# Masking the row-max scores of a causal attention by a VectorE minimum in PSUM instead of by TensorE mask products

## The chip, the cores and the metric
One core of one Trainium2 chip runs the whole program, a decoder stack of four layers at batch 2, sequence 1024, width 128. The metric is the device time of one execution in microseconds. Before the change it is 2020.6 us, the median of 3 runs (2019.37 to 2026.57).

## The reference, cut to what matters
Only the first attention is touched. It has 16 heads of 64 columns and runs, for each batch, each head:

```python
sim = jnp.einsum('bhid,bhjd->bhij', q, k)
causal_mask = jnp.triu(jnp.ones((n, n), dtype=bool), k=1)
sim = jnp.where(causal_mask, mask_value, sim)            # mask_value = -finfo.max
attn = jax.nn.softmax(sim.astype(jnp.float32), axis=-1)
out = jnp.einsum('bhij,bhjd->bhid', attn, v)
adj = jnp.clip(adj + jnp.eye(n), 0.0, 1.0)               # adj = attn
deg = jnp.sum(adj, axis=-1, keepdims=True)
for l in range(GNN_DEPTH):                               # 2
    h = feats @ gnn_w[l] + gnn_b[l]
    h = jnp.einsum('bij,bjd->bid', adj, h) / deg
    feats = jax.nn.gelu(h + feats, approximate=False)
out = out + (feats @ lin_w + lin_b)                      # then @ Wo and a layer norm
```

n is 1024, feats starts as v. The softmax needs the maximum of each row over the keys up to the row's own place.

## The kernel before, in words
The work is cut into 16 units, each a pair of heads of one batch; `for_units` lets each engine run its own list of instructions for a unit g (`body`), in a hardware loop over the middle six pairs of a batch. Engines meet only through semaphores. The rows of a unit are 8 tiles of 128.

A unit needs its scores twice. First with rows on the partitions, to find the row maxima (`row_scores`, `row_part` on TensorE, `row_max` on VectorE): for row tile `it` the products of Q with the keys 0 to (it+1)*128 go to PSUM, and VectorE reduces them. Then with keys on the partitions, as three products of split parts plus one that subtracts the row's maximum (`score`), for the exponentials `E` that ScalarE writes (line 486). Both use the same two PSUM buffers `ring0` and `ring1` of 1024 columns (two heads of 512; `pair(r)`). Row tiles 0 to 3 fit into one buffer and alternate; tiles 4 to 7 have two halves, the first in ring0, the second, with the diagonal block, in ring1. A part is announced by `rowmax_ready`; the part that uses the same buffer next waits for `max_done` of the reduce. So TensorE is at most two parts ahead of VectorE.

In the diagonal block the keys above the row's own place must not count. TensorE sees to that with one more product per head after the scores: identity times a 128x128 bf16 matrix that holds -1e38 above the diagonal (`identb`, `mask`, line 580), added in PSUM. For the second kind of scores it is done otherwise: VectorE takes a minimum in place in PSUM with `cap`, 3e38 where the entry stands and -1e38 where it is masked (`own_score`, line 887).

The row maxima of unit g+1 are made inside the body of unit g. TensorE's order there is written out by hand: tile 0 behind the values of the next unit, tiles 1 and 2 behind the first output mix, then the second layer's aggregations (`aggregate(F1, ...)`, line 643) with tiles 3 to 7 between them, `max_rows` (line 610: the maxima turned into a row), the first scores of the next unit (`score`, line 628), and the second layer's products (`product2`, line 695). VectorE's order is: sums and `scaled`/`out1` (lines 917, 937) with tile 0 between, `set_own` (16 instructions on the diagonal of E, line 931), tiles 1 to 5, `out2` (line 917), tiles 6 and 7, `own_score` of the next unit. For tiles 4 to 7 the two partial maxima are joined and widened by one VectorE instruction from SBUF to SBUF (`widen_high`, tile `mw`, line 879). GpSimd meanwhile runs a quotient, two bias additions and the additions of `out2`, each 128x512 (lines 356, 365, 400, 350, 371).

Of the kernel before, what the change touches and what calls it, by code (L numbers as in the profile page):

```python
# [5 lines left out]
ALU = mybir.AluOpType  # L6
# [3 lines left out]
BF16 = mybir.dt.bfloat16  # L10
# [3 lines left out]
P = 128  # L14
# [4 lines left out]
ST = SEQ // P  # L19
# [157 lines left out]
def l0_attention(nc, d, x, xnT, ident, norm):  # L177

    with ExitStack() as ctx:
        sb, pb, sem = scope(nc, ctx, "l0a")  # L180
# [6 lines left out]
        maskf = sb("maskf", [P, P])  # L187
        wo, go = sb("wo", [P, PAIRS, P]), sb("go", [P, P])
        const_in, w_in = sem("const_in"), sem("w_in")
        consts = ((maskf[:, :], d["cmask"]), (wo[:, :, :], d["wo"]), (go[:, :], d["gout"].partition_broadcast(P)),  # L190
# [5 lines left out]
        mask = sb("mask", [P, P], BF16)  # L196
        identb = sb("identb", [P, P], BF16)
# [42 lines left out]
        pool_step = sem("pool_step")  # L240
        cast_done, q_ready, k_ready, vw_ready = sem("cast_done"), sem("q_ready"), sem("k_ready"), sem("vw_ready")
# [9 lines left out]
        ua_kept, gl_kept, capped = sem("ua_kept"), sem("gl_kept"), sem("capped")  # L251
# [16 lines left out]
        def hi(h):  # L268

            return slice(h * DH, (h + 1) * DH)  # L270
# [7 lines left out]
        def pair(r):  # L278

            return ring[r][:, :].rearrange("p (h c) -> p h c", c=512)  # L280
# [21 lines left out]
        block = ctx.enter_context(nc.Block(no_gpsimd_drain=True))  # L302
# [31 lines left out]
        def _(pool):  # L334
# [3 lines left out]
            pool.wait_ge(pool_step, 2)  # L338
            pool.affine_select(out=cap[:, :], in_=cap[:, :], compare_op=ALU.is_ge, fill=-1.0e38, base=0,
                               pattern=[[1, P]], channel_multiplier=-1).then_inc(pool_step, 1)  # L340
            pool.wait_ge(const_in, NCONST)
# [203 lines left out]
        def _(pe):  # L545
            pe.wait_ge(const_in, NCONST)
            pe.wait_ge(cast_done, 6)
            pe.wait_ge(pool_step, 3)
# [24 lines left out]
            def row_part(u, it, r, c0, c1):  # L573

                for h in range(2):
                    mm = pe.matmul(pair(r)[:, h, 0:c1 - c0], QH[hi(h), it * P:(it + 1) * P], KH[hi(h), c0:c1],  # L576
                                   start=True, stop=c1 <= it * P)
                if c1 > it * P:
                    for h in range(2):
                        mm = pe.matmul(pair(r)[:, h, it * P - c0:c1 - c0], identb[:, :], mask[:, :], start=False, stop=True)  # L580
                mm.then_inc(rowmax_ready, 1)
# [262 lines left out]
        def _(dve):  # L844
            dve.wait_ge(const_in, NCONST)
            dve.wait_ge(pool_step, 3)
            dve.tensor_copy(mask[:, :], maskf[:, :]).then_inc(cast_done, 1)
            dve.tensor_copy(identb[:, :], ident[:, :]).then_inc(cast_done, 1)
# [12 lines left out]

            def row_max(u, *tiles):
                for it in tiles:
                    w = (it + 1) * P
                    if it < 4:
                        dve.wait_ge(rowmax_ready, u * NMAX + (it + 1))
                        dve.tensor_reduce(mx[:, :, it], pair(it % 2)[:, :, 0:w], AX_X, ALU.max).then_inc(max_done, 1)
                    else:
                        n = 4 + 2 * (it - 4)
                        dve.wait_ge(rowmax_ready, u * NMAX + (n + 1))  # L870
                        dve.tensor_reduce(mx[:, :, it], pair(0)[:, :, :], AX_X, ALU.max).then_inc(max_done, 1)  # L871
                        dve.wait_ge(rowmax_ready, u * NMAX + (n + 2))
                        dve.tensor_reduce(mxb[:, :, it - 4], pair(1)[:, :, 0:w - 512], AX_X, ALU.max).then_inc(max_done, 1)
                        widen_high(u, it)
# [21 lines left out]
            def first():  # L896
                keep_q_lo(0)
                keep_k_lo(0)
                row_max(0, *range(ST))
                own_score(0, 0)  # L900
# [2036 lines left out]
```

## Time and profile before
| | |
|---|---|
| median of 3 runs | 2020.6 us (2019.37 to 2026.57) |
| the profiled execution: its time, its span | 2026.7 us, 2025.0 us |
| TensorE (PE), VectorE (DVE), ScalarE (ACT), GpSimd (POOL) busy | 76%, 64%, 37%, 43% of the span |
| the first attention's row scores and maxima run | from 43 to 923 us |
| DMA | 28 GB/s on the mean |

Times in rows are microseconds from the start of the span; "mean ns of one" is the mean duration. An instruction's busy time can overlap that of its neighbour on the same engine, so the cost of one in a chain is read from start to start. A number in square brackets at a row's end is the time for which the engine was idle before it, with the instruction that released it.

### The profile page before, as it was taken

The numbers are of one execution on the slowest core, as the hardware profiler recorded it, in microseconds if no ns is written. First come the engines' busy times: TensorE is split into PE (matmuls) and PEld (weight loads), VectorE is DVE, ScalarE is ACT, GpSimd is POOL, SyncE is SP. The second block draws the span as 40 slices with busy tenths as digits, with TensorE's granted clock in tenths as the row PEclk, the third lists the DMA queues.
The fourth block names the chain that finished last, engine by engine and source line by source line (L and its number), as shares of the span: only waits on it lengthen the run. The fifth ranks groups of instructions, "written<-read, shape, count | busy, mean of one in ns | idle before, by whom it ended". The sixth has DMA issues, their size and how long they took to land. (4 is left out here: it accounts for less than half of the span.)

```text
span 2025.0 us, 25396 instructions
## 1 busy us (share of the span) xinstructions
PE 1533.3 (76%) x8233; PEld 898.2 (44%) x8233; DVE 1292.2 (64%) x2908; ACT 757.3 (37%) x1151; POOL 878.7 (43%) x574
## 2 busy tenths in 40 slices
PE   3999999999899999998666869552185736767547
PEld 2555455555555555555424546341164212222436
DVE  5567777777577777676675245677124669989514
ACT  1444444444344444544253213210021455445012
POOL 0455665566455566656200400000512028898133
PEclk9899999999999999998878759765587859888658
DMA  1000000000000000000000000005112012211232
GB/s 52 6 6 0 5 5 5 5 5 6 1 6 6 5 5 5 5 0 1 13 0 7 1 6 16 14 7 187 39 40 67 19 36 83 82 64 52 49 120 71
DMA packets 47259, 55.96 MB, mean 28 GB/s; under 512 B 8816, under 2 KB 34696, under 8 KB 46912
## 3 DMA queue, kind: packets, MB, share of 16 engines
q1 hardware_dynamic: 44272, 49.00, 8.0%
q0 software_dynamic: 2912, 6.02, 0.9%
q8 instruction: 39, 0.64, 0.1%
q14 instruction: 36, 0.29, 0.0%
HBM read 42.85 MB, written 12.15 MB: 27 GB/s over the span
## 5 line engine op out<-in xcount | busy, mean ns | idle before, releaser
L486 ACT ACTIVATE l0a_E<-l0a_ring 128x1024 f32<-128x1024 f32 x192 | 150.4, 810 | 185.9 <-DVE l0a_scrap L892 178.8
L384 POOL TENSOR_TENSOR l0a_acc<-l0a_acc,l0a_E 128x1536 f32<-128x1536 f32 (+2 forms) x96 | 201.0, 2093 | 9.1
L2602 PE MATMUL mx_ysum<-mx_hst,main_ident 128*128 128x512 f32 x256 | 143.9, 698 | 50.0 <-POOL mx_hst L2690 43.2
L2703 POOL TENSOR_TENSOR mx_dBu<-mx_XI,mx_BB 128x1024 f32<-128x1024 f32 x64 | 137.6, 2177 | 83.7 <-DVE mx_XI L2766 83.7
L643 PE MATMUL l0a_agg<-l0a_E,l0a_VH 128*64 128x512 f32 (+3 forms) x768 | 150.5, 498 | 0.1
L643 PE MATMUL l0a_agg<-l0a_E,l0a_F 128*64 128x512 f32 (+3 forms) x768 | 148.9, 505 | 0.8 <-ACT l0a_F L447 0.8
L2675 ACT ACTIVATE mx_dA<-mx_DT,mx_A 128x512 f32<-128x512 f32 x128 | 88.2, 690 | 98.8 <-DVE mx_hst L2783 98.8
L887 DVE TENSOR_TENSOR l0a_ring<-l0a_ring,l0a_cap 128x256 f32<-128x256 f32 x128 | 55.0, 430 | 108.6 <-PE l0a_ring L633 108.6
L925 DVE RECIPROCAL l0a_AT<-l0a_RB 128x128 f32<-128x128 f32 x128 | 111.9, 920 | 1.5
L2602 PEld LDWEIGHTS mx_ysum<-mx_hst,main_ident 128*128 128x128 f32 x256 | 53.9, 219 | 120.9 <-POOL mx_hst L2690 61.9
L384 POOL TENSOR_TENSOR l0a_acc<-l0a_E 128x1792 f32<-128x1792 f32 x16 | 64.4, 4024 | 81.0 <-ACT l0a_E L486 81.0
L628 PE MATMUL l0a_ring<-l0a_QH,l0a_KH 64*128 64x512 f32 (+3 forms) x384 | 81.4, 420 | 19.2 <-ACT l0a_E L486 17.4
L165 PE MATMUL n_turned<-main_ident,n_xn 128*128 128x128 f32 x96 | 26.0, 460 | 92.0 <-DVE n_xn L135 92.0
L576 PE MATMUL l0a_ring<-l0a_KH,l0a_QH 64*128 64x512 f32 (+3 forms) x384 | 80.3, 439 | 18.7 <-DVE l0a_mx L871 5.5
L2783 DVE TENSOR_TENSOR_SCAN mx_hst<-mx_dA,mx_hst,mx_dBu 128x512 f32<-128x512 f32 x64 | 82.1, 1283 | 7.5 <-DVE mx_hst L2783 0.5
L628 PEld LDWEIGHTS l0a_ring<-l0a_QH,l0a_KH 64*128 64x128 f32 x384 | 36.5, 187 | 109.7 <-ACT l0a_E L486 67.4
L371 POOL TENSOR_TENSOR l0a_S<-l0a_S,l0a_F1B 128x512 f32<-128x512 f32 x32 | 40.9, 1279 | 99.7 <-DVE l0a_S L917 99.7
L389 POOL TENSOR_TENSOR l0a_T<-l0a_VW,l0a_small 128x512 f32<-128x512 f32 x32 | 33.4, 1043 | 111.2 <-DVE l0a_small L913 111.2
L871 DVE TENSOR_REDUCE l0a_mx<-l0a_ring 128x2 fp32r<-128x1024 f32 x64 | 78.1, 1220 | 5.4 <-PE l0a_ring L576 5.4
L892 DVE SCALAR_TENSOR_TENSOR l0a_scrap<-l0a_ring,main_ident 128x128 f32<-128x128 f32 x256 | 74.6, 291 | 8.9
L576 PEld LDWEIGHTS l0a_ring<-l0a_KH,l0a_QH 64*128 64x128 f32 x384 | 35.2, 186 | 101.1 <-DVE l0a_mx L871 32.4
L2783 DVE TENSOR_TENSOR_SCAN mx_hst<-mx_dA,mx_dBu 128x512 f32<-128x512 f32 x64 | 77.4, 1210 | 2.5 <-POOL mx_dBu L2703 2.5
(493 smaller groups left out, 3764.4 us busy)
## 6 DMA issues: line engine op xcount, KB each, us to landing
mx_BB<-mx_brows SPq DMA_DIRECT2D x32, 512.0 KB, 3.6
me_W<-in_f_w SPq DMA_DIRECT2D x16, 256.0 KB
l0a_wp<-in_wqkv SPq DMA_DIRECT2D x16, 192.0 KB
moe_Wg<-in_f_wg SPq DMA_DIRECT2D x8, 256.0 KB
moe_Wu<-in_f_wu SPq DMA_DIRECT2D x8, 256.0 KB
moe_Wd<-in_f_wd SPq DMA_DIRECT2D x8, 256.0 KB
moe_Y<-rt_zeros SPq DMA_DIRECT2D x2, 1024.0 KB, 11.0
e_back<-moe_Y SPq DMA_DIRECT2D x8, 256.0 KB, 4.7
```

The lines of the kernel that those rows point to most:

```text
L384: pool.tensor_tensor(dst, src, E[:, :, ecol[jt]:ecol[jt] + w], ALU.add).then_inc(acc_done, 1)
L486: act.activation(E[:, :, at:at + n], pair(k % 2)[:, :, 0:n], ACT.Exp).then_inc(exp_done, 1)
L576: mm = pe.matmul(pair(r)[:, h, 0:c1 - c0], QH[hi(h), it * P:(it + 1) * P], KH[hi(h), c0:c1], start=True, stop=c1 <= it * P)
L628: pe.matmul(out[:, h, 0:n], a[hi(h), keys], b[hi(h), at], start=a is KH and b is QH, stop=False, skip_group_check=True)
L643: mm = pe.matmul(agg[c][cols, lo - 512 * c:512], feats[:, jt, cols], E[:, h, at + lo:at + hi], start=(jt == 0), stop=(jt == 4 * c + 3), sk ...
L871: dve.tensor_reduce(mx[:, :, it], pair(0)[:, :, :], AX_X, ALU.max).then_inc(max_done, 1)
L892: dve.scalar_tensor_tensor(scrap[:, :], pair(k % 2)[:, h, 0:P], 1.0, ident[:, :], ALU.mult, ALU.mult, accum_out=eii[:, jt, h:h + 1]).then_ ...
L925: dve.reciprocal(AT[:, t], RB[:, t]).then_inc(inv_done, 1)
L2602: mm = pe.matmul(ysum[h][:, c * 512:(c + 1) * 512], ident[:, :], hst[:, k % DEEP, c * 512:(c + 1) * 512], start=(n == 0), stop=(n == NS - ...
L2675: act.activation(dA[:, c * 512:(c + 1) * 512], DT[:, h, b * SEQ + c * 512:b * SEQ + (c + 1) * 512], ACT.Exp, scale=A[:, h, n:n + 1]).then_ ...
L2703: pool.tensor_tensor(dBu[:, k % DEEP, :], du_of(h, b), BB[:, q % 3, :], ALU.mult).then_inc(dBu_ready, 1)
L2783: dve.tensor_tensor_scan(hst[:, k % DEEP, half], dA[:, half], dBu[:, k % DEEP, half], hst[:, k % DEEP, 511:512] if c else 0.0, ALU.mult, A ...
```

## The change
The mask products are gone, with their operands: the input mask's load, the bf16 casts of mask and identity. In their place stands a matrix `rowcap` made by GpSimd at the start, and in `row_max` a VectorE minimum of the diagonal block with it (`cap_row`), followed by a wait on its own end, before the reduce of that tile.

```diff
-        maskf = sb("maskf", [P, P])
-        consts = ((maskf[:, :], d["cmask"]), (wo[:, :, :], d["wo"]), ...
+        consts = ((wo[:, :, :], d["wo"]), ...
-        mask = sb("mask", [P, P], BF16)
-        identb = sb("identb", [P, P], BF16)
+        rowcap = sb("rowcap", [P, P])
...
             pool.memset(cap[:, :], 3.0e38).then_inc(pool_step, 1)
-            pool.wait_ge(pool_step, 2)
+            pool.memset(rowcap[:, :], 3.0e38).then_inc(pool_step, 1)
+            pool.wait_ge(pool_step, 3)
...
+            pool.affine_select(out=rowcap[:, :], in_=rowcap[:, :], compare_op=ALU.is_ge, fill=-1.0e38, base=0,
+                               pattern=[[-1, P]], channel_multiplier=1).then_inc(pool_step, 1)
...
                     mm = pe.matmul(pair(r)[:, h, 0:c1 - c0], QH[hi(h), it * P:(it + 1) * P], KH[hi(h), c0:c1],
-                                   start=True, stop=c1 <= it * P)
-                if c1 > it * P:
-                    for h in range(2):
-                        mm = pe.matmul(pair(r)[:, h, it * P - c0:c1 - c0], identb[:, :], mask[:, :], start=False, stop=True)
+                                   start=True, stop=True)
                 mm.then_inc(rowmax_ready, 1)
...
-            dve.tensor_copy(mask[:, :], maskf[:, :]).then_inc(cast_done, 1)
-            dve.tensor_copy(identb[:, :], ident[:, :]).then_inc(cast_done, 1)
...
+            def cap_row(u, it, block):
+                dve.tensor_tensor(block, block, rowcap[:, :].unsqueeze(1).broadcast_to([P, 2, P]), ALU.min).then_inc(row_capped, 1)
+                dve.wait_ge(row_capped, u * ST + (it + 1))
...
                     if it < 4:
                         dve.wait_ge(rowmax_ready, u * NMAX + (it + 1))
+                        cap_row(u, it, pair(it % 2)[:, :, it * P:w])
...
                         dve.wait_ge(rowmax_ready, u * NMAX + (n + 2))
+                        cap_row(u, it, pair(1)[:, :, it * P - 512:w - 512])
                         dve.tensor_reduce(mxb[:, :, it - 4], pair(1)[:, :, 0:w - 512], AX_X, ALU.max).then_inc(max_done, 1)
```

VectorE's order before, in the body of a unit, from `set_own` (line 931) to the widening of tile 5; the three reduces of line 867 are tiles 1 to 3:

```order
L931 SCALAR_TENSOR_TENSOR l0a_E<-main_ident,l0a_small,l0a_E 128x128 x16
L867 TENSOR_REDUCE l0a_mx<-l0a_ring 128x2 x3
L871 TENSOR_REDUCE l0a_mx<-l0a_ring 128x2
L873 TENSOR_REDUCE l0a_mxb<-l0a_ring 128x2
L879 TENSOR_TENSOR l0a_mw<-l0a_mx,l0a_mxb 128x128
L871 TENSOR_REDUCE l0a_mx<-l0a_ring 128x2
L873 TENSOR_REDUCE l0a_mxb<-l0a_ring 128x2
L879 TENSOR_TENSOR l0a_mw<-l0a_mx,l0a_mxb 128x128
```

The same place in the changed kernel, to the widening of tile 4 (lines 933, 868, 872, 875 and 881 are the former 931, 867, 871, 873 and 879):

```order
L933 SCALAR_TENSOR_TENSOR l0a_E<-main_ident,l0a_small,l0a_E 128x128 x16
L859 TENSOR_TENSOR l0a_ring<-l0a_ring,l0a_rowcap 128x2x128
L868 TENSOR_REDUCE l0a_mx<-l0a_ring 128x2
L859 TENSOR_TENSOR l0a_ring<-l0a_ring,l0a_rowcap 128x2x128
L868 TENSOR_REDUCE l0a_mx<-l0a_ring 128x2
L859 TENSOR_TENSOR l0a_ring<-l0a_ring,l0a_rowcap 128x2x128
L868 TENSOR_REDUCE l0a_mx<-l0a_ring 128x2
L872 TENSOR_REDUCE l0a_mx<-l0a_ring 128x2
L859 TENSOR_TENSOR l0a_ring<-l0a_ring,l0a_rowcap 128x2x128
L875 TENSOR_REDUCE l0a_mxb<-l0a_ring 128x2
L881 TENSOR_TENSOR l0a_mw<-l0a_mx,l0a_mxb 128x128
```

A minimum now stands ahead of each reduce that holds a diagonal block; the order is otherwise the same. TensorE's order before, from tile 3 (ring1) over both halves of tile 4 to the second layer's product:

```order
L576 MATMUL l0a_ring1<-l0a_KH,l0a_QH 128x512 x2
L580 MATMUL l0a_ring1<-l0a_mask,l0a_identb 128x128 x2
L643 MATMUL l0a_agg1<-l0a_E,l0a_F1 64x512 x2
L596 REGISTER_ALU
L576 MATMUL l0a_ring0<-l0a_KH,l0a_QH 128x512 x2
L596 REGISTER_ALU
L576 MATMUL l0a_ring1<-l0a_KH,l0a_QH 128x128 x2
L580 MATMUL l0a_ring1<-l0a_mask,l0a_identb 128x128 x2
L643 MATMUL l0a_agg1<-l0a_E,l0a_F1 64x512 x2
L695 MATMUL l0a_prod<-l0a_gnn_lin,l0a_U2 128x128 x4
```

And in the changed kernel (lines 577, 641 and 693 are the former 576, 643 and 695):

```order
L577 MATMUL l0a_ring1<-l0a_KH,l0a_QH 128x512 x2
L641 MATMUL l0a_agg1<-l0a_E,l0a_F1 64x512 x2
L577 MATMUL l0a_ring0<-l0a_KH,l0a_QH 128x512 x2
L577 MATMUL l0a_ring1<-l0a_KH,l0a_QH 128x128 x2
L641 MATMUL l0a_agg1<-l0a_E,l0a_F1 64x512 x2
L693 MATMUL l0a_prod<-l0a_gnn_lin,l0a_U2 128x128 x4
```

Only the products of line 580 are gone; the parts stand where they stood.

## Rows read from the trace of the kernel before

**Rows 1.** Windows: stretch, length, busy (instructions) of PE, PEld, DVE, ACT, POOL; clock, DMA share, GB/s.
```profile
59.00:115.00 56.00, 51.22 (x314) 28.14 (x314) 31.13 (x81) 25.00 (x37) 27.72 (x16) 0.95 0.02 6
171.00:227.00 56.00, 54.05 (x342) 29.61 (x338) 40.70 (x93) 27.16 (x42) 33.99 (x21) 1.00 0.02 5
```

**Rows 2.** Grouped lines, 0 to 1000 us: busy us, mean ns, idle before.
```profile
L580 PE MATMUL l0a_ring<-l0a_mask,l0a_identb 128*128 128x128 bf16 x256 | 37.0, 227 | 0.0
```

**Rows 3.** One line's instructions (887, 879): count, ns min/median/max, first and last start.
```profile
L887 DVE TENSOR_TENSOR l0a_ring<-l0a_ring,l0a_cap x128: 405/433/433, 58.0 to 944.3; 128x256 f32<-128x256 f32 x128
...
L879 DVE TENSOR_TENSOR l0a_mw<-l0a_mx,l0a_mxb x64: 291/293/1397, 49.1 to 922.6; 128x128 fp32r<-128x128 f32 x64
```

**Rows 4.** Timeline of PE, 427 to 453.5 us: start, duration, line, operation.
```profile
438.06 0.29 PE L580 MATMUL l0a_ring<-l0a_mask,l0a_identb 128*128 128x128 bf16 x2
438.28 1.08 PE L643 MATMUL l0a_agg<-l0a_E,l0a_F 128*64 128x512 f32 x4
439.29 0.71 PE L576 MATMUL l0a_ring<-l0a_KH,l0a_QH 64*128 64x512 f32 x4
...
440.14 1.08 PE L643 MATMUL l0a_agg<-l0a_E,l0a_F 128*64 128x512 f32 x4
...
442.24 0.61 PE L576 MATMUL l0a_ring<-l0a_KH,l0a_QH 64*128 64x512 f32 x4
...
447.11 0.50 PE L576 MATMUL l0a_ring<-l0a_KH,l0a_QH 64*128 64x512 f32 x2 [0.33 <-DVE l0a_mx L871]
447.98 0.50 PE L576 MATMUL l0a_ring<-l0a_KH,l0a_QH 64*128 64x512 f32 x2 [0.36 <-DVE l0a_mxb L873]
...
452.73 0.50 PE L628 MATMUL l0a_ring<-l0a_QH,l0a_KH 64*128 64x512 f32 x2
```

**Rows 5.** Timeline of DVE, 427 to 453.5 us.
```profile
430.35 0.68 DVE L917 TENSOR_TENSOR l0a_S<-l0a_prod,l0a_small 128x512 f32<-128x512 f32 x1
431.34 0.69 DVE L937 TENSOR_TENSOR l0a_S<-l0a_S,l0a_T 128x512 f32<-128x512 f32 x1 [0.31 <-POOL l0a_T L392]
...
436.15 1.55 DVE L867 TENSOR_REDUCE l0a_mx<-l0a_ring 128x2 fp32r<-128x512 f32 x2
438.39 1.23 DVE L867 TENSOR_REDUCE l0a_mx<-l0a_ring 128x2 fp32r<-128x1024 f32 x1 [0.69 <-PE l0a_ring L580]
439.83 1.23 DVE L871 TENSOR_REDUCE l0a_mx<-l0a_ring 128x2 fp32r<-128x1024 f32 x1 [0.22 <-PE l0a_ring L576]
440.97 0.41 DVE L873 TENSOR_REDUCE l0a_mxb<-l0a_ring 128x2 fp32r<-128x256 f32 x1
441.42 1.40 DVE L879 TENSOR_TENSOR l0a_mw<-l0a_mx,l0a_mxb 128x128 fp32r<-128x128 f32 x1
442.78 1.23 DVE L871 TENSOR_REDUCE l0a_mx<-l0a_ring 128x2 fp32r<-128x1024 f32 x1
...
444.64 0.68 DVE L879 TENSOR_TENSOR l0a_mw<-l0a_mx,l0a_mxb 128x128 fp32r<-128x128 f32 x1
...
445.85 1.21 DVE L871 TENSOR_REDUCE l0a_mx<-l0a_ring 128x2 fp32r<-128x1024 f32 x1
...
451.31 0.43 DVE L887 TENSOR_TENSOR l0a_ring<-l0a_ring,l0a_cap 128x256 f32<-128x256 f32 x1 [0.47 <-PE l0a_ring L633]
451.78 0.29 DVE L892 SCALAR_TENSOR_TENSOR l0a_scrap<-l0a_ring,main_ident 128x128 f32<-128x128 f32 x1
```

**Rows 6.** Timeline of POOL, 445 to 447 us.
```profile
445.14 1.32 POOL L350 TENSOR_TENSOR l0a_VB<-l0a_VH,l0a_gnnb 128x512 f32<-128x512 f32 x1
446.42 1.26 POOL L371 TENSOR_TENSOR l0a_S<-l0a_S,l0a_F1B 128x512 f32<-128x512 f32 x1
```

**Rows 7.** Timeline of DVE, 43 to 59 us, the first preparation.
```profile
44.92 2.73 DVE L867 TENSOR_REDUCE l0a_mx<-l0a_ring 128x2 fp32r<-128x512 f32 x3 [0.87 <-PE l0a_ring L580]
...
57.97 0.43 DVE L887 TENSOR_TENSOR l0a_ring<-l0a_ring,l0a_cap 128x256 f32<-128x256 f32 x1 [1.16 <-PE l0a_ring L633]
```

More of the change, by code:

```diff
@@ L186, in l0_attention @@
         linb = sb("linb", [P, 1])
-        maskf = sb("maskf", [P, P])
         wo, go = sb("wo", [P, PAIRS, P]), sb("go", [P, P])
         const_in, w_in = sem("const_in"), sem("w_in")
-        consts = ((maskf[:, :], d["cmask"]), (wo[:, :, :], d["wo"]), (go[:, :], d["gout"].partition_broadcast(P)),
+        consts = ((wo[:, :, :], d["wo"]), (go[:, :], d["gout"].partition_broadcast(P)),
                   (gnnb[0][:, :], d["gnn_row"][0:1, :].partition_broadcast(P)),
@@ L250, in l0_attention @@
         agg1_ready, ut_kept, at_done, inv_done = sem("agg1_ready"), sem("ut_kept"), sem("at_done"), sem("inv_done")
-        ua_kept, gl_kept, capped = sem("ua_kept"), sem("gl_kept"), sem("capped")
+        ua_kept, gl_kept, capped, row_capped = sem("ua_kept"), sem("gl_kept"), sem("capped"), sem("row_capped")
         p1_ready, s1a_done, s1_done = sem("p1_ready"), sem("s1a_done"), sem("s1_done")
@@ L546, in _ @@
             pe.wait_ge(const_in, NCONST)
-            pe.wait_ge(cast_done, 6)
-            pe.wait_ge(pool_step, 3)
+            pe.wait_ge(cast_done, 4)
+            pe.wait_ge(pool_step, 5)
             def composite(u):
@@ L845, in _ @@
             dve.wait_ge(const_in, NCONST)
-            dve.wait_ge(pool_step, 3)
-            dve.tensor_copy(mask[:, :], maskf[:, :]).then_inc(cast_done, 1)
-            dve.tensor_copy(identb[:, :], ident[:, :]).then_inc(cast_done, 1)
+            dve.wait_ge(pool_step, 5)
             dve.tensor_copy(identr[:, :], ident[:, :]).then_inc(cast_done, 1)
```

## The prediction
> **What bounds the kernel now.** I read the windows first, then the grouped lines, then three timelines of one unit (TensorE, VectorE, GpSimd) side by side. The change touches only the first attention. One head pair (a "unit") takes 56.0 us there, and from 115 to 507 us every unit repeats the same pattern. In such a window TensorE is busy 54.05 of 56 us at full clock and VectorE 40.70 [rows 1]. Averages say: TensorE is the bound, VectorE has 15 us to spare. But the averages don't decide, since the changed instructions lie in one stretch of the unit, from 430 to 453 us in the unit shown. There TensorE makes the row scores of tile 5, VectorE reduces them, TensorE may overwrite the same PSUM buffer with tile 7 (or the next half), and so on: a ring of two buffers. The reader is to see in [rows 4] that TensorE, which has almost no idle time, already waits twice in this stretch for VectorE's maxima (0.33 and 0.36 us before the halves of tile 7), and in [rows 5] that VectorE works nearly without a gap: from 436.15 to 451 us its only waits of note are 0.69 and 0.22 us. Here VectorE is the bound or within 1 us of it, and it is this stretch that gets new VectorE work.
>
> **What goes.** 256 mask products (two for each of 128 tiles), 37.0 us of TensorE busy [rows 2]. Busy counts overlap: from the mask's start at 438.06 to the next product at 438.28 is 0.22 us [rows 4], so a tile gives back 0.21 to 0.22 us, 1.7 us a unit, if TensorE is what it waits for. Also gone: one load of 64 KB and two casts ahead of the first unit, beside which the start now has one memset and one affine_select on GpSimd; a few tenths each way, taken as 0 (bounds -0.5 and +0.5).
>
> **What comes.** One VectorE minimum per tile, in place in PSUM on 128x256, 128 in all, each with a wait on its own end before the reduce behind it. An instruction of the same shape and operands stands in the trace: the minimum with `cap` takes 405/433/433 ns (min/median/max of 128) and the next instruction starts 0.47 us after it (451.31 to 451.78); others do so after 0.45, so I take 0.46. Reduces without such a wait start the next one 0.09 us before they end (439.83 + 1.23 against 440.97) [rows 3, 5]. So a unit gets 8 x 0.46 = 3.7 us of VectorE work and its TensorE loses 1.7 us.
>
> The Trainium skill (VectorE: DVE Perf Modes, The DRAIN you can't avoid) says that a semaphore behind each VectorE instruction costs nothing extra over the flush that comes anyway. The two gaps above disagree by 0.12 us an instruction. By that page of the Trainium skill a cap would cost 0.34 us and, with two caps on the path behind the lock wait below, a unit some 0.24 us less and the whole 3.6 us less; I go by the row.
>
> **The chain through one unit**, all times on the clock of the unit shown [rows 4 to 6]:
> 1. Tile 0: its cap delays the product with the sums at 430.35 by 0.46, to an end at 431.49; the addition behind it stood at 431.34 waiting 0.31 us for GpSimd, so it starts near 431.42: only 0.08 us late. The row maxima of tiles 1 and 2 start at 436.15 + 0.08 = 436.23.
> 2. Tiles 1 and 2 take 0.60 and 0.87 us (1.55 for both with the overlap), with caps 0.46 more each: 438.62. Before, tile 3 could start only at 438.39, when its mask product was done; the idle 0.69 us is eaten. Tile 3: 438.62 + 0.46 + 1.23 = 440.31, before 438.39 + 1.23 = 439.62.
> 3. TensorE's second half of tile 4 needs the buffer of tile 3. It ran at about 439.7 without waiting and now starts at 440.36; behind it are the aggregation, the second layer's product and tile 5. Without the mask, and with 0.26 us for the short half (an estimate from the 0.71 us that both halves take), the aggregation starts at 440.62 instead of 440.14, and tile 5 at 442.72 instead of 442.24.
> 4. VectorE takes up tile 5 0.54 us after TensorE starts it (439.29 to 439.83, and 442.24 to 442.78), so at 443.26. Reduce 1.14, cap 0.46, reduce 0.72: the widening instruction (`mw`, line 879) comes up at 445.58 instead of 444.64.
> 5. This one has a wait that the order doesn't show. It takes 291/293/1397 ns [rows 3]: in the unit shown 1.40 us for tile 4 and 0.68 for tile 5, and both times it ends 0.18 us after a GpSimd instruction has ended (445.14 + 0.18 = 445.32 = 444.64 + 0.68). With the shift of 0.08 the GpSimd boundary lies at 445.22; the instruction now comes 0.36 us too late for it and waits for the next, 446.42 + 0.08 = 446.50, so it ends at 446.68: 1.36 us later than before. (For tile 4 the same wait works the other way: it absorbs the delay, since it was waiting anyway.)
> 6. Tile 6 starts at 445.85 + 1.35 = 447.20; first half 1.13, cap 0.46, second half 0.94: done at 449.73. TensorE's second half of tile 7 starts at 449.78, not 447.98: 1.80 late, less the mask gone behind it, 1.6 us. Everything that follows (the scores at 452.73, the exponentials, the next unit) hangs on TensorE's order and carries this on; nothing later in the unit has slack to give it back, with 1.95 us of idle in 56.
>
> What is queued behind the new waits: on VectorE the maxima themselves, on TensorE everything, since the row scores stand between aggregations in one order. GpSimd and ScalarE start later by the same amount and wait as before.
>
> **Sum.** 15 units prepare the next one's maxima: 15 x 1.6 = 24.0 us. The first preparation has nothing beside it: 3.7 us of caps, of which 0.87 us is covered by VectorE's idle time before tile 1 and 1.16 by that before its first score [rows 7]: 1.7 us. The two first units of the batches have no quotient on GpSimd, so less of step 5, but more idle on TensorE; taken at the same price. Together +25.7 us. The profiled execution took 2026.7 us, 6.1 above the median 2020.6; 2052.4 by its own time, 2046 by the median's. Bounds of a cap: from 0.34 (duration less overlap) to 0.55, near the row's 0.46, since shape and memories are the same. Those of the chain: no less than what the maxima of tile 3 force (0.4 us a unit), no more than 7 caps in line less 1.7 of masks and less the 0.9 us of idle eaten, plus one lock wait of 1.3: 1.9 us.
>
> **Rivals.**
> - *The lock wait is missed.* Step 5 rests on 0.36 us. If the widening of tile 5 catches the earlier boundary, it ends at 445.40, tile 6 starts only 0.15 us late, and what remains is two caps in tiles 6 and 7 less their masks: 0.4 us a unit, 15 x 0.4 + 1.7 = 8 us, 2029. For it: the margin is less than one cap. Against it: three independent shifts (0.08, 0.48, 0.46) add up to it. The Trainium skill (SBUF — State Buffer, Who interferes with whom) gives the mechanism: a VectorE instruction with two SBUF inputs and a GpSimd instruction that reads SBUF block each other for a whole instruction, whoever came first. By that rule the caps, with one SBUF input, are free of it; the row of 433 ns at most agrees. Chance 18%.
> - *VectorE's spare time covers it, faster.* If each tile's cap fits into the time in which TensorE does its aggregation, the masks' 128 x 0.21 = 27 us come back: 1994. For it: 54.05 busy of 56, and 15 us spare. Against it: TensorE waits for the maxima of tile 7 already. It decides at tile 3: the cap would have to end the reduce by 439.7, 0.6 us earlier than I work out. 6%.
> - *The clock falls.* The granted clock is 1.00 (2.4 GHz) in the window with 54.05 us busy; the window 59 to 115 with 51.22 busy shows 0.95, but its idle gaps lie beside work that ran at full clock [rows 1]. Gaps of 1 us each in the stretch might bring 1.2 GHz in each unit; 3 us of matrix work at that level would take up to 3 us longer, 15 x 3 = 45 more, 2091. The Trainium skill (TensorE: Matmul & The Clock Gate, A second HAM failure mode) reports a kernel in which such short idles between groups did that. 4%.
> - The minimum is as costly as said but the mask is left in place somewhere: excluded, no such product is left in this attention.
>
> **How the numbers follow.** My forecast 62%, range of its own 2040 to 2054; missed lock wait 18%, faster 6%, clock 4%, and 10% for units that settle between (2033 to 2040) or a second lock wait (up to 2062). 0.5% is 10 us, about what a measurement tells from no change. Faster 0.06; within 0.5% (up to 2031) the missed lock wait, nearly all of it: 0.17; slower 0.77. The range from 2028 to 2060 leaves out the faster case and the clock.
>
> **What would show it.** In the changed trace: units of 57.6 us; the cap at 0.43 us; TensorE waiting for the row maxima (lines of the row scores) some 3 us a unit instead of 0.7, first at the second half of tile 4; the widening at up to 1.3 us for tile 5; TensorE busy 1.7 us less a unit; clock 1.00. Wrong if units stay at 56 us or less, or if the widening of tile 5 is short.

## The result, and the profile after

The changed kernel takes 2058.03 us (median of 4, 2056.62 to 2062.06), the kernel before on the same chip 2021.13. The ratio is 1.0181, with a 95% interval from 1.0157 to 1.0205: slower by 37 us, where the sum said 26. The time lies inside the stated range of 2028 to 2060, close to its upper end, and above the 2040 to 2054 that the forecast gave as its own. The execution profiled after took 2058.1 us, with a span of 2056.4.

The first look is at the windows, the form in which [rows 1] stand: stretch, length, busy (instructions) of PE, PEld, DVE, ACT, POOL, granted clock, DMA share, GB/s. Each window here is one unit of the changed kernel, from one copy of the row sums (line 910) to the next.

```profile
380.79:438.51 57.72, 52.66 (x323) 28.75 (x323) 43.47 (x102) 27.31 (x44) 33.93 (x21) 1.00 0.02 5
321.58:380.79 59.21, 54.13 (x323) 29.25 (x323) 43.58 (x102) 27.27 (x44) 33.97 (x21) 0.97 0.02 4
694.93:755.10 60.17, 55.33 (x323) 29.83 (x323) 43.58 (x102) 27.22 (x44) 33.98 (x21) 0.94 0.02 5
```

There are three kinds of unit. The first is what the forecast worked out: 57.72 us, where the kernel before has 56.00, at full clock, with VectorE busy 2.8 us more and TensorE 1.4 us less. The second is 1.5 us longer and its clock is 0.97, the third 2.5 us longer at 0.94. I call a stretch at a granted clock of 0.50 (1.2 GHz) a dip. From the first to the last copy there are 15 units. Eleven are regular; the first of each batch, the one with the change of batch and the last one have a pattern of their own. Of the 11, five are of the first kind, four of the second, two of the third. In the kernel before all 11 are alike, between 55.96 and 56.03 us at full clock.

The timeline of PE over one undisturbed unit answers to [rows 4]; the two units lie 13.67 us apart (tile 0 of the row scores starts at 428.73 before and at 442.40 here).

```profile
445.21 1.12 PE L729 MATMUL l0a_prod<-l0a_FT,l0a_gnn_lin 128*128 128x512 f32 x2 [0.96 <-DVE l0a_S L919]
...
454.14 0.33 PE L577 MATMUL l0a_ring<-l0a_KH,l0a_QH 64*128 64x128 f32 x2 [1.00 <-DVE l0a_mx L868]
454.39 1.08 PE L641 MATMUL l0a_agg<-l0a_E,l0a_F 128*64 128x512 f32 x4
...
456.49 0.62 PE L577 MATMUL l0a_ring<-l0a_KH,l0a_QH 64*128 64x512 f32 x4
...
458.32 0.50 PE L577 MATMUL l0a_ring<-l0a_KH,l0a_QH 64*128 64x512 f32 x2 [0.20 <-DVE l0a_mx L872]
459.39 0.45 PE L577 MATMUL l0a_ring<-l0a_KH,l0a_QH 64*128 64x384 f32 x2 [0.57 <-DVE l0a_mxb L875]
...
462.18 0.50 PE L577 MATMUL l0a_ring<-l0a_KH,l0a_QH 64*128 64x512 f32 x2 [0.75 <-DVE l0a_mx L872]
463.51 0.49 PE L577 MATMUL l0a_ring<-l0a_KH,l0a_QH 64*128 64x512 f32 x2 [0.83 <-DVE l0a_mxb L875]
...
468.10 0.51 PE L626 MATMUL l0a_ring<-l0a_QH,l0a_KH 64*128 64x512 f32 x2
```

TensorE now waits 1.00 us ahead of the second half of tile 4 and 0.20 and 0.57 ahead of the halves of tile 6, where it did not wait before, and 0.75 and 0.83 ahead of the halves of tile 7, where it was 0.33 and 0.36. That makes 3.35 us of waiting for row maxima a unit instead of 0.69. The wait of 0.96 us in the first row is for sums that stand behind the minimum of tile 0 on VectorE; before, it was 0.42. The last row stood at 452.73 before; 468.10 - 13.67 is 454.43, 1.70 us later.

The timeline of DVE in the same unit answers to [rows 5]:

```profile
450.01 0.42 DVE L859 TENSOR_TENSOR l0a_ring<-l0a_ring,l0a_rowcap 128x256 f32<-128x256 f32 x1
450.46 0.69 DVE L868 TENSOR_REDUCE l0a_mx<-l0a_ring 128x2 fp32r<-128x512 f32 x1
...
456.04 0.61 DVE L881 TENSOR_TENSOR l0a_mw<-l0a_mx,l0a_mxb 128x128 fp32r<-128x128 f32 x1
457.04 1.23 DVE L872 TENSOR_REDUCE l0a_mx<-l0a_ring 128x2 fp32r<-128x1024 f32 x1 [0.38 <-PE l0a_ring L577]
...
459.37 1.03 DVE L881 TENSOR_TENSOR l0a_mw<-l0a_mx,l0a_mxb 128x128 fp32r<-128x128 f32 x1
460.32 0.68 DVE L919 TENSOR_TENSOR l0a_S<-l0a_prod,l0a_small 128x512 f32<-128x512 f32 x1
460.92 1.21 DVE L872 TENSOR_REDUCE l0a_mx<-l0a_ring 128x2 fp32r<-128x1024 f32 x1
```

and the same of POOL to [rows 6]:

```profile
457.75 2.50 POOL L351 TENSOR_TENSOR l0a_VB<-l0a_VH,l0a_gnnb 128x512 f32<-128x512 f32 x2
461.07 1.26 POOL L372 TENSOR_TENSOR l0a_S<-l0a_S,l0a_F1B 128x512 f32<-128x512 f32 x1 [0.83 <-DVE l0a_S L919]
```

The minimum takes 0.42 us and the reduce behind it starts 0.45 us after it. The widening of tile 4 (line 881) takes 0.61 us, where it was 1.40: it comes later and ends within 0.2 us of the same place. That of tile 5 comes up at 459.37 and ends at 460.40, 0.15 us after the two GpSimd instructions of which the first started at 457.75. The second of them had started at 458.98, 0.39 us before the widening came up. For the two instructions' forms over the whole run, the source view gives what answers to [rows 3]:

```profile
L859 DVE TENSOR_TENSOR l0a_ring<-l0a_ring,l0a_rowcap x128: 415/422/433, 42.6 to 960.1; 128x256 f32<-128x256 f32 x128
...
L881 DVE TENSOR_TENSOR l0a_mw<-l0a_mx,l0a_mxb x64: 291/293/1044, 50.0 to 961.8; 128x128 fp32r<-128x128 f32 x64
```

[rows 2] have no counterpart, the mask products are gone. The first preparation, on DVE, answers to [rows 7]:

```profile
43.91 0.43 DVE L859 TENSOR_TENSOR l0a_ring<-l0a_ring,l0a_rowcap 128x256 f32<-128x256 f32 x1 [0.41 <-PE l0a_ring L577]
...
59.19 0.43 DVE L889 TENSOR_TENSOR l0a_ring<-l0a_ring,l0a_cap 128x256 f32<-128x256 f32 x1 [0.56 <-PE l0a_ring L631]
```

The idle time ahead of tile 1 has shrunk from 0.87 to 0.41 us and that ahead of the first score from 1.16 to 0.56; the first score is capped at 59.19 instead of 57.97, 1.2 us later. But the row scores also started earlier in this execution, at 42.24 instead of 43.04. From there to the capped score it is 16.95 us instead of 14.93.

Where a unit is longer, windows inside it show where. In the unit that starts at 321.58:

```profile
343.00:346.70 3.70, 2.11 (x12) 0.85 (x12) 3.63 (x6) 0.60 (x1) 1.58 (x2) 1.00 0.00 0
346.70:350.10 3.40, 3.40 (x16) 1.45 (x16) 3.15 (x5) 0.00 (x0) 0.00 (x0) 0.50 0.00 0
350.10:353.60 3.50, 3.50 (x28) 2.81 (x30) 1.76 (x7) 2.18 (x3) 0.00 (x0) 1.00 0.00 0
```

The first window holds TensorE's waits for tile 7: it is busy 2.11 of 3.70 us. Right behind it TensorE works without a gap, but at 0.50, 1.2 GHz; then the clock is back.

**The account.** From the first to the last copy of the row sums the kernel before takes 864.2 us (90.18 to 954.37), the changed one 902.4 (91.65 to 994.06): +38.2. The six regular units with a dip are together 11.0 us longer than six of 57.71 would be. The other 27.2 us are 1.81 for each of the 15 units, where a regular one without a dip has 1.71. Not all of them belong to the instructions: the last unit of the 15 is 2.8 us longer than before, and it holds 9.1 us at half clock where the kernel before holds 5.4. A second profile of the changed kernel (the last run below) gives by the same working +38.3, of which 13.5 are dips of seven units and 24.8 the rest. Ahead of the first copy 1.5 us are added, so the first profile has +39.7. The spans differ by less, 31.4, since the untouched rest of the program took 1070.6 us in one profiled execution and 1062.3 in the other. It is the same code: in the eleven runs below it takes between 1059.4 and 1069.7 us. So the units are the measure here, and the medians of several runs; a pair of single spans is not.

### The profile page after: what moved, and what is told of

Read it like the earlier page. It is cut to its first block and busy times, and to the rows that moved or that the text cites. A ratio compares the mean times of both kernels' runs of the same rounds, so it can differ in the third digit from the quotient of the medians.

```text
span 2056.4 us, 25096 instructions
## 1 busy us (share of the span) xinstructions
PE 1518.6 (74%) x7977; PEld 886.7 (43%) x7977; DVE 1337.8 (65%) x3034; ACT 758.9 (37%) x1151; POOL 878.5 (43%) x576
## 5 line engine op out<-in xcount | busy, mean ns | idle before, releaser
L641 PE MATMUL l0a_agg<-l0a_E,l0a_F 128*64 128x512 f32 (+3 forms) x768 | 157.9, 532 | 0.8 <-ACT l0a_F L448 0.8
L577 PE MATMUL l0a_ring<-l0a_KH,l0a_QH 64*128 64x512 f32 (+3 forms) x384 | 81.0, 445 | 60.6 <-DVE l0a_mxb L875 21.3
```

Source lines behind the costliest of these rows:

```text
L641: mm = pe.matmul(agg[c][cols, lo - 512 * c:512], feats[:, jt, cols], E[:, h, at + lo:at + hi], start=(jt == 0), stop=(jt == 4 * c + 3), sk ...
```

## The experiments

Each kernel ran with its own profile and several timed executions beside the kernel before. "Unit" is the length of a regular unit without a dip; dips are counted in the 11 regular units of the one profiled execution. The ratio is to the kernel before on the same chip, whose median was 2021.8 us beside the runs from "neither" to "minima on tiles 4 to 7", 2025.1 beside those from "GpSimd shifted" to "neither, tensor_scalar", and 2020.1 beside the last two and "changed, again". Across these groups the ratios compare, not the medians.

| run | unit us | units with a dip | median us | ratio to before (95%) |
|---|---|---|---|---|
| before | 56.00 | 0 | 2021 | |
| changed | 57.71 | 6 | 2058.0 | 1.0181 (1.0157 to 1.0205) |
| changed, again | 57.7 | 7 | 2059.1 | 1.0191 (1.0158 to 1.0224) |
| neither | 54.93 | 0 | 2007.5 | 0.9921 (0.9902 to 0.9940) |
| both | 57.87 | 0 | 2051.8 | 1.0135 (1.0113 to 1.0157) |
| minima on tiles 0 to 3 | 57.40 | 0 | 2044.2 | 1.0119 (1.0093 to 1.0144) |
| minima on tiles 4 to 7 | 56.31 | 0 | 2033.0 | 1.0044 (1.0029 to 1.0058) |
| GpSimd shifted | 56.97 | 3 | 2053.3 | 1.0135 (1.0104 to 1.0165) |
| filler products | 57.72 | 2 | 2054.2 | 1.0150 (1.0126 to 1.0174) |
| widening by tensor_scalar | 58.01 | 0 | 2050.5 | 1.0144 (1.0116 to 1.0173) |
| neither, tensor_scalar | - | 11 | 2058.0 | 1.0163 (1.0139 to 1.0187) |
| neither, ScalarE widens | 54.32 | 0 | 1996.9 | 0.9887 (0.9863 to 0.9912) |
| minima, ScalarE widens | 57.33 | 0 | 2038.4 | 1.0089 (1.0060 to 1.0117) |

**Neither.** The two calls of the minimum are taken out of the changed kernel, so the row maxima are taken over the keys above the diagonal too. This holds for the two other kernels with "neither" as well (with tensor_scalar, and with ScalarE widening); the scores of the second kind keep their mask.

```diff
-                        cap_row(u, it, pair(it % 2)[:, :, it * P:w])
...
-                        cap_row(u, it, pair(1)[:, :, it * P - 512:w - 512])
```

> The changed kernel without its minima: neither mask products nor minima, so the row maxima include the keys above the diagonal of the last block (any bound at or above the true maximum serves the softmax). Theory A (the added time is VectorE's chain from tile 1 to tile 7, and TensorE's part of the change is a real gain of 1.7 us a unit): units of 54.6 us instead of 56.0, total 1999 us, and no dips of the granted clock in the repeated units. Rival B (VectorE's chain of maxima bounded the unit already, so products taken from TensorE bring nothing): units of 55.8 us, total 2017.

The units are 54.93 us, 1.07 shorter than before; the products were a real cost, but only two thirds of the 1.7 us came back. Of the rest, part is VectorE's: here TensorE waits for maxima four times in the stretch, 1.07 us in all, where it was 0.69 before. Rival B is refuted, and my value was 0.3 too low. The total, 2007.5, was expected at 1999.

**Both.** Mask products and minima in every tile. The diff is against the kernel before.

```diff
                 if c1 > it * P:
                     for h in range(2):
                         mm = pe.matmul(pair(r)[:, h, it * P - c0:c1 - c0], identb[:, :], mask[:, :], start=False, stop=True)
...
+                        cap_row(u, it, pair(it % 2)[:, :, it * P:w])
...
+                        cap_row(u, it, pair(1)[:, :, it * P - 512:w - 512])
```

> Mask products and minima both: TensorE as busy as before, VectorE as in the changed kernel. Theory A with the clock (TensorE's idle gaps in the changed kernel bring the dips to 1.2 GHz that cost 1.5 us each in 7 of its units): units of 57.9 us, 0.2 longer than the changed kernel's undisturbed 57.7, but no or few dips, total 2051, below the changed kernel's 2058. Rival C (the dips come by chance or from elsewhere): as many dips, total 2061.

A window of one unit:

```profile
380.60:438.47 57.87, 54.15 (x339) 29.59 (x339) 43.22 (x102) 27.26 (x44) 33.98 (x21) 1.00 0.02 5
```

TensorE does all the work that it did before, VectorE all that it does in the changed kernel, and the unit is only 0.16 us longer than the changed one: removing the products gains next to nothing once the minima are there, since TensorE then waits. With the masks the wait ahead of the first half of tile 7 is 0.34 us, where the changed kernel has 0.75; that ahead of the second half is 0.83 in both. And although a unit without a dip is longer, the kernel is faster than the changed one (1.0135 against 1.0181, intervals that just touch at 1.0157), and no regular unit has a dip: from the first to the last copy it takes 892.1 us, the changed one 902.4. That is the clock's part of the loss, shown from the other side.

**Half the tiles each.** The lists of tiles with a minimum and of tiles with a mask product are split. The diff, against the kernel before, is that of the kernel with minima on tiles 0 to 3; in the other one the two lists are exchanged. What feeds the mask products (the load and the two casts) is back in both.

```diff
-                if c1 > it * P:
+                if c1 > it * P and it in (4, 5, 6, 7):
...
+            CAPS = (0, 1, 2, 3)
...
+                if it in CAPS:
```

> Minima for row tiles 0 to 3, mask products for 4 to 7. Theory A: the four minima make the maxima of tile 3 0.7 us late, tile 5's widening arrives at 445.33 on the clock of the unit shown, misses the GpSimd boundary at 445.22 by 0.1 and ends near 446.68: unit 57.3 us (+1.3), total 2042. If it just catches the boundary: 56.4. Rival D (each minimum costs its share, half of the 1.7): 56.85 us, total 2035.

> Mask products for row tiles 0 to 3, minima for 4 to 7. Theory A: tile 4's delay is absorbed by the wait for GpSimd that its widening has anyway; tile 5's widening arrives at 445.10, just before the boundary at 445.14, and ends at 445.32 as before; what is left are the minima of tiles 6 and 7 less a mask: unit 56.25 us, total 2026. If it misses the boundary: 57.6, as the changed kernel. Rival D: 56.85 us, total 2035.

57.40 and 56.31 us against 57.3 and 56.25 expected. The totals are 2044.2 and 2033.0 against 2042 and 2026: the second is 7 us above. The unit doesn't account for that; in its profile the first unit and the one with the change of batch have dips (6.8 and 3.4 us) that the kernel before doesn't have there. Four minima cost 1.40, the other four 0.31 us, with the same instructions in the same number, and the two together are the 1.71 of the changed kernel; rival D (0.85 each) is refuted. What differs is the widening of tile 5. With the minima on tiles 0 to 3 the DVE timeline has

```profile
454.11 0.68 DVE L886 TENSOR_REDUCE l0a_mxb<-l0a_ring 128x2 fp32r<-128x512 f32 x1
454.82 1.29 DVE L892 TENSOR_TENSOR l0a_mw<-l0a_mx,l0a_mxb 128x128 fp32r<-128x128 f32 x1
```

and with those on tiles 4 to 7

```profile
450.59 0.69 DVE L886 TENSOR_REDUCE l0a_mxb<-l0a_ring 128x2 fp32r<-128x512 f32 x1
451.31 0.29 DVE L892 TENSOR_TENSOR l0a_mw<-l0a_mx,l0a_mxb 128x128 fp32r<-128x128 f32 x1
```

the same instruction, once 1.29 us and once 0.29, which is 1.00 of the 1.09 us between the two.

**GpSimd shifted.** One more GpSimd addition of 0.59 us, whose result nobody reads.

```diff
+        SHIFT = 1
...
                 if prev is not None:
+                    for _ in range(SHIFT):
+                        pool.tensor_tensor(filler[:, :], VB[:, 0, :].unsqueeze(1).broadcast_to([P, 2, P])[:, :, 0:96], VH[:, 0, :].unsqueeze(1).broadcast_to([P, 2, P])[:, :, 0:96], ALU.add).then_inc(filled, 1)
                     quotient(g, prev)
```

> The changed kernel with one more GpSimd addition (128x192, into a tile that nothing reads, about 0.6 us) ahead of the quotient, in units that have one, so that the following GpSimd instructions end 0.6 us later. Theory A (tile 5's widening waits 0.7 us because it misses a GpSimd boundary by 0.37 us): the widening of tile 5 now comes just before the boundary and takes 0.3 to 0.5 us instead of 1.03; units of 57.1 us instead of 57.7 although work was added, total 2047 with fewer dips of the clock. Rival (the widening is slow for a reason of its own): 57.7 or longer, 2058 to 2067.

Eight of the 11 regular units got shorter by 0.74 us through added work. DVE and POOL around the widening of tile 5 in one of them, and PE behind it:

```profile
457.35 0.29 DVE L886 TENSOR_TENSOR l0a_mw<-l0a_mx,l0a_mxb 128x128 fp32r<-128x128 f32 x1
```

```profile
456.13 2.64 POOL L354 TENSOR_TENSOR l0a_VB<-l0a_VH,l0a_gnnb 128x512 f32<-128x512 f32 x2
```

```profile
459.42 0.50 PE L582 MATMUL l0a_ring<-l0a_KH,l0a_QH 64*128 64x512 f32 x2
460.76 0.50 PE L582 MATMUL l0a_ring<-l0a_KH,l0a_QH 64*128 64x512 f32 x2 [0.83 <-DVE l0a_mxb L880]
```

The widening now falls between the two instructions of this pair and takes 0.29 instead of 1.03 us. The other three units (at 376.98, 637.42 and 697.97) are 59.5, 60.6 and 59.5 us long, and in each of them the same widening takes 1.41 or 1.42 us:

```profile
397.85 1.41 DVE L886 TENSOR_TENSOR l0a_mw<-l0a_mx,l0a_mxb 128x128 fp32r<-128x128 f32 x1
```

```profile
401.04 0.50 PE L582 MATMUL l0a_ring<-l0a_KH,l0a_QH 64*128 64x512 f32 x2 [1.14 <-DVE l0a_mx L877]
402.37 0.79 PE L582 MATMUL l0a_ring<-l0a_KH,l0a_QH 64*128 64x512 f32 x2 [0.83 <-DVE l0a_mxb L880]
```

It comes up 20.86 us after the start of its unit in all 11. The second GpSimd instruction of the pair starts at 20.855 to 20.864 in the three units and at 20.866 to 20.884 in the eight: a few hundredths of a microsecond decide over 1.1. That settles step 5: the wait is for the GpSimd instruction under way. The clock follows. The three units with the long widening, in which TensorE waits ahead of both halves of tile 7, are the three with a dip; the eight others have neither. The total is 6 us above what was expected, on a chip where the kernel before is some 4 us slower too; the three units are 8.6 us longer than three of 56.97, and the change of batch has a long widening and a dip as well.

**Filler products.** Products of the identity with itself, into a bank that is free, where TensorE waits: five ahead of the second half of tile 4 and three ahead of that of tile 6, though not in the first preparation.

```diff
+        FILL = {4: 5, 6: 3}
...
                         for r in range(2):
+                            if r == 1 and not (isinstance(u, int) and u == 0) and it in FILL:
+                                for _ in range(FILL[it]):
+                                    pe.matmul(turn[:, 0:P], identr[:, :], identr[:, :], start=True, stop=True)
```

> The changed kernel with products nobody reads (identity by identity, 128x128, into the bank `turn` while it is free) where TensorE waits for maxima: 5 ahead of the second half of tile 4, where it idles 1.0 us, 3 ahead of that of tile 6, where it idles 0.57. Clock theory (the dips to 1.2 GHz come from TensorE's idle gaps in this stretch): no dips, units stay at 57.7, total 2050. Rival (the dips have nothing to do with these gaps): dips as before, 2058 or above.

Units of 57.72, as expected, and two dips instead of six or seven, at a ratio of 1.0150 instead of 1.0181 and 1.0191. The gaps that were filled (1.00 and 0.57 us, now 0.28 and none) are not those right ahead of the dips, at tile 7, for which I had no free bank; these are still 0.77 and 0.83. No dips were expected, fewer are not none, and the intervals overlap: this run leans the clock theory's way and doesn't settle it.

**The widening by tensor_scalar.** Two instructions with one tensor from SBUF and a scalar pointer each. The tile `mxb` becomes plain fp32 with it.

```diff
-                dve.tensor_tensor(mw[:, it, :, :], spread(mx[:, :, it], shape), spread(mxb[:, :, it - 4], shape),
-                                  ALU.max).then_inc(mw_high, 1)
+                for h in range(2):
+                    ins = dve.tensor_scalar(mw[:, it, h, :], spread(mx[:, h, it], [P, DH]), mxb[:, h, it - 4:it - 3], None, ALU.max)
+                ins.then_inc(mw_high, 1)
```

> The changed kernel with the widening of tiles 4 to 7 written as two VectorE tensor_scalar instructions (one per head, one tensor from SBUF, the other maximum as a scalar pointer) in the place of one with two tensors from SBUF. Theory A with the lock rule: neither waits for GpSimd any more, each takes 0.17 to 0.25 us; tile 5's widening is done 0.65 us earlier, those of 6 and 7 take 0.15 us more: units of 57.2 us, total 2050. Rival (the wait is for something else than the second input): the new instructions take up to 1.3 us too, units of 57.8 us or more.

This failed: 58.01 us. The source view shows why:

```profile
L882 DVE TENSOR_SCALAR l0a_mw<-l0a_mx,l0a_mxb x128: 245/254/1321, 49.6 to 954.8; 128x64 fp32r<-128x64 f32 x128
```

These instructions can take 1.32 us as well. It is now the second one of tile 4 that does so in every regular unit, while those of tile 5 take 0.25. The rival named it rightly: one tensor input alone doesn't free an instruction. It fits what the Trainium skill says (SBUF — State Buffer, Who interferes with whom), that tensor_scalar can run in a mode that takes both ports and then contends with GpSimd; I had used only half of that rule, and no run here shows the mode itself. The total of 2050.5 agrees with the expected 2050 by luck: the units are 0.8 us longer than expected, and none has a dip. With units 0.3 us longer than in the changed kernel and TensorE no busier (52.8 us), it isn't slower than that kernel (1.0144 against 1.0181, overlapping intervals). TensorE waits 0.83 us ahead of the second half of tile 7 here but only 0.14 ahead of the first.

**Neither, tensor_scalar.** The same edit in the kernel with neither.

> Neither mask products nor minima, and the widening as two one-input instructions. Theory A: the waits for GpSimd of 0.7, 0.15 and 0.8 us (tiles 4, 5 and 6 in the kernel with neither) go; TensorE's remaining waits in the stretch shrink from 1.8 to about 1.2 us: units of 54.4 us instead of 54.93, total 2000. Rival: unchanged, 54.9 and 2007.

The worst miss of the study: 2058.0 us where 2000 was expected and 2007.5 was there without the edit. On PE:

```profile
400.00 1.04 PE L577 MATMUL l0a_ring<-l0a_KH,l0a_QH 64*128 64x512 f32 x4 [1.04 <-DVE l0a_mx L871]
...
404.28 1.66 PE L577 MATMUL l0a_ring<-l0a_KH,l0a_QH 64*128 64x512 f32 x4 [1.64 <-DVE l0a_mx L871]
```

TensorE waits 1.04 and then, in most units, 1.64 us for maxima behind widenings of up to 1.32 us, and every one of the 11 regular units has a dip of the clock (0.50 for 3.4 to 10.2 us of it); they take 58.0 to 61.3 us. The other form of four widenings a unit took the ratio from 0.9921 to 1.0163, some 49 us. A regular unit is on the mean 3.8 us longer than with neither: TensorE is busy 2.1 us more, with the same products at the lower clock, and idle 1.7 us more.

**ScalarE widens.** VectorE joins the two partial maxima by a reduce of 2x2 elements, ScalarE spreads the result.

```diff
...
-                dve.tensor_tensor(mw[:, it, :, :], spread(mx[:, :, it], shape), spread(mxb[:, :, it - 4], shape),
-                                  ALU.max).then_inc(mw_high, 1)
+                dve.tensor_reduce(mxh[:, :, it - 4], mxp[:, :, it - 4, :], AX_X, ALU.max).then_inc(joined, 1)
...
+                    act.wait_ge(joined, u * 4 + (it - 3))
+                    act.activation(mw[:, it, :, :], spread(mxh[:, :, it - 4], [P, 2, DH]), ACT.Copy).then_inc(mw_high, 1)
```

> Neither mask products nor minima, and for tiles 4 to 7 VectorE joins the two partial maxima by a reduce of 2x2 elements (one input) and ScalarE widens them with a copy, so that no VectorE instruction of this stretch can wait for GpSimd. Theory A: units of 54.3 us (54.93 with the widening that waits), total 1999. Rival (the widening is slow for another reason than GpSimd, or ScalarE is now late for TensorE): 54.9 or longer, 2007 or above.

Without masks and minima:

```profile
308.00:362.33 54.33, 52.46 (x323) 28.95 (x323) 38.68 (x93) 28.17 (x48) 33.91 (x21) 1.00 0.02 5
```

54.32 us a unit and 1996.9 us, where 54.3 and 1999 were expected, and faster than both kernels of this study, by 1.1% over the kernel before (0.9863 to 0.9912). The softmax allows it: what is subtracted must only bound the row, and not by so much that the exponentials vanish, which depends on the inputs; the masked keys get their zero from the minimum that the second kind of scores has anyway.

> The changed kernel with its minima, and the widening split between VectorE's small reduce and ScalarE as in the run before. Theory A (0.75 us of the changed kernel's unit is the widening of tile 5 waiting for GpSimd): units of 56.9 us instead of 57.7, of which the pure minima cost 0.9 over the kernel before; total 2045. Rival: 57.7, 2058.

With the minima: 57.33 us, 0.38 shorter than the changed kernel, where 0.8 was expected. The wait of tile 5 is gone, but a new one came: on PE and ACT at the unit's end stand

```profile
463.17 0.82 PE L619 MATMUL l0a_turn<-l0a_identr,l0a_mw 128*128 128x128 f32 x4
464.14 1.16 PE L704 MATMUL l0a_prod<-l0a_gnn_lin,l0a_U 128*128 128x128 f32 x8 [0.16 <-ACT l0a_U L446]
```

```profile
463.30 0.31 ACT L460 ACTIVATE l0a_mw<-l0a_mxh 128x128 fp32r<-128x128 f32 x1 [2.65 <-DVE l0a_mxh L891]
463.51 0.58 ACT L446 ACTIVATE l0a_U<-l0a_agg 128x512 f32<-128x512 f32 x1
```

From the row of the maxima to the next product it is 0.97 us, before 0.50: ScalarE's widening of tile 7 comes late and holds up its copy of the aggregate behind it. The total, 2038.4, is lower than the 2045 expected. That fits the missing dips: the expected value was 13 us under the changed kernel's, whose time holds them. Ahead of the first half of tile 7 TensorE doesn't wait here, ahead of the second it waits 0.80 us.

**The changed kernel again.**

> The changed kernel once more, for the dips of the granted clock. If they hang on where the chip looks at TensorE's idle gaps at tile 7 and not on a fault of one execution: again undisturbed units of 57.7 us, with several units of 59.2 or 60.2 in the profile, perhaps in other places, and a median of 2055 to 2060. Rival (the dips of the first profile were a freak of it): no dips, and a median that the profile with dips does not match, under 2050.

2059.1 us, seven of 11 regular units with a dip, some in other places (380.69 and 440.87 in the first batch), and undisturbed ones of 57.66 to 57.76. The dips are the kernel's, their places are not.

## Why the prediction was right, and where a term was missing

**The bound.** The stretch from tile 1 to tile 7 decides, not the average over the unit: right. The minima on four tiles cost 1.40 us and on four others 0.31; busy totals can't say that. TensorE's waits for maxima were forecast at some 3 us a unit and are 3.35.

**What goes.** 1.7 us of products a unit: the busy time fell by 1.4 to 1.5, the unit in the kernel with neither by 1.07. In the changed kernel none of it is seen (both against changed: 0.16).

**The minimum, steps 1 to 4.** 0.43 us and 0.46 to the next were forecast by [rows 3, 5], 0.42 and 0.45 measured. With 13.67 us added, the forecast's times for the second half of tile 4, the aggregation, tile 5 and the widening are 454.03, 454.29, 456.39 and 459.25; measured 454.14, 454.39, 456.49 and 459.37. They are late by 0.10 to 0.12 us, as is the first of the minima (450.01 against 449.90), so this is step 1's delay and not the chain's: the addition behind tile 0 is 0.18 us late where 0.08 was worked out. An instruction behind a wait on the one before starts 0.03 us after that one's end (450.01 + 0.42 against 450.46), and one without it 0.08 us ahead of it (450.46 + 0.69 against 451.07). The Trainium skill (VectorE: DVE Perf Modes, The DRAIN you can't avoid) says that the semaphore costs nothing extra; by that the prediction's estimate was 0.34 in place of 0.45. The measurement decides against it for this pair, a minimum and a wait on its own end.

**Step 5, the wait for GpSimd.** Forecast end 460.35, measured 460.40. Shown by three runs: 1.29 against 0.29 us in the two halves, and 0.29 or 1.41 with GpSimd shifted, where the unit lost 0.74 us with the short one. Of the 1.71 us a unit, 0.74 are this wait. The rival that it is missed had 18%; the widening came up 0.39 us behind the start of the GpSimd instruction, where 0.36 was worked out.

**Step 6 and the sum.** 1.6 us a unit forecast, 1.71 measured. The 15 units came to 27.2 us in one profile and 24.8 in the other, dips of the regular units left out (24.0 forecast); in the first, those at the batches' starts and ends had 1.2 to 2.8 instead of 1.6, dips partly included. Ahead of the first copy it is 1.5 us more, forecast 1.7; that is close by luck, since the first preparation itself got 2.0 us longer and started 0.8 us earlier. Such a start is not the change's doing for certain: it lies between 41.87 and 42.98 in the other runs. By the windows of the first profile the change costs 39.7 us against a forecast of 25.7: 11.0 of the 14 are the clock, 3 the instructions with the last unit's clock. The medians say 37, with the rest of the program in them, which varies by more than the 3 us between the two figures.

**The clock.** This is the term that was missing from the sum, and because of it the time lies above the forecast's own 2040 to 2054 and close to the end of the stated range; that it still lies inside is owed to room left for other things. I gave the falling clock 4%, as an alternative to the forecast and at 3 us in every unit. It came beside it: 1.5 us for a dip of 3.4 us in a unit, 2.5 for one of 6.8, in half of the units, 11.0 and 13.5 us in the two profiles. I had argued that gaps beside work at full clock do no harm [rows 1]. That window does hold a single wait of 1.86 us at full clock (at 96.98), but nothing like the pair of waits at tile 7, which were 0.33 and 0.36 us before [rows 4]. What TensorE waited ahead of the two halves of tile 7, against the dips in the 11 regular units (counted in one profiled execution of each kernel, two of the changed one):

| kernel | waits us | dips |
|---|---|---|
| before | 0.33, 0.36 | 0 |
| both | 0.34, 0.83 | 0 |
| minima on tiles 0 to 3 | 0.94, 0.36 | 0 |
| neither | 0.17, 0.37 | 0 |
| neither, ScalarE widens | none, 0.33 | 0 |
| minima on tiles 4 to 7 | none, 0.83 | 0 |
| widening by tensor_scalar | 0.14, 0.83 | 0 |
| minima, ScalarE widens | none, 0.80 | 0 |
| GpSimd shifted, eight units | none, 0.83 | 0 |
| GpSimd shifted, three units | 1.14, 0.83 | 3 |
| filler products | 0.77, 0.83 | 2 |
| changed, and again | 0.75, 0.83 (0.60 to 0.66 in units with 6.8 us) | 6 and 7 |

The kernel with neither and tensor_scalar has another pattern, 1.04 us ahead of tile 6 and mostly 1.64 ahead of tile 7, and a dip in each unit. In the kernels of the table the dips begin 23.8 to 25.2 us after the start of the unit; the first of the two waits ends at 23.7 (24.1 in the shifted kernel), the second at 25.0 (25.4). So the dips go with the pair of waits at tile 7, and not with the idle time of the whole unit: TensorE idles 5.2 us in a unit of the tensor_scalar kernel, which has no dip, and 5.1 in one of the changed kernel. That these waits bring the dips is shown by the shifted kernel, whose two kinds of unit part at the widening of tile 5 and the wait behind it, ahead of the dip, and by the kernel with both, faster in spite of longer units. Which of the units with the same waits get one is open, and so is why.

**Faster by spare time** (6%) is refuted at the place it named: the reduce of tile 3 ends at 454.09 - 13.67 = 440.42, not by 439.7.

## What to carry to other kernels

Moving work from a busy engine to one with idle time pays only if the idle time lies where the work goes; lay the two engines' timelines of the stretch side by side, and follow the buffers between them. Look at each instruction whose maximum is several times its median: its wait can turn a delay of 0.4 us into one of 1.3, or absorb it. Gaps of TensorE can cost more than their length: where the clock fell behind them, each such unit lost 1.5 or 2.5 us more, so a sum over waits alone can come out too low.

## What I had not expected of the hardware

- A VectorE tensor_scalar on 64 columns, fp32 in SBUF, took 245 to 1321 ns beside GpSimd work.
- With GpSimd shifted, one and the same widening took 0.29 us in eight units and 1.41 in three, with GpSimd starts that lie within 0.03 us of each other.
- A dip of the granted clock to 0.50 for 3.4 us cost a unit 1.5 us, one of 6.8 us 2.5.
- The kernel with neither masks nor minima gained 14 us, and the same kernel with an instruction form that waits for GpSimd lost some 49 us again.
- The untouched rest of the program varied by 11 us (1059.4 to 1070.6) between profiled executions, more than several of the effects studied here.
